# The variance of the decoder attention's row norm: root and reciprocal on two engines, or one power on GpSimd

## The reference, cut to what matters

```
x = _layernorm(x + _L1_attn_ref(x, ...), axis=-1)
x = _layernorm(x + _L1_xattn_ref(ctx_1024, ctx_1024, x, mask, ...), axis=-1)

def _layernorm(x, axis=-1, eps=1e-05):
    m = jnp.mean(x, axis=axis, keepdims=True)
    v = jnp.var(x, axis=axis, keepdims=True)
    return (x - m) / jnp.sqrt(v + eps)
```

## Time and profile before

| | |
|---|---|
| median of 3 runs | 3104.47 us (3103.09 to 3105.31) |
| profiled execution, first to last instruction (its span; no other time of it is listed) | 3103.9 us |
| PE busy | 2762.8 us, 89% of the span |
| DVE busy | 2047.4 us, 66% |
| ACT busy | 1633.0 us, 53% |
| POOL busy | 290.6 us, 9% |
| the stream in the span | about 1390 to 2653 us |
| mean granted TensorE clock over the span | 0.944 |

### The profile page before, as it was taken

The page is one execution under the profiler, slowest core; times in us unless marked ns, Lnnn a source line. Parts: engine busy times, 40 slices in busy tenths (PEclk is TensorE's granted clock), DMA queues, the critical chain, the costliest instruction groups (busy, mean ns, idle before and its releaser), DMA issues. The chain is left out here.

```text
span 3103.9 us, 86016 instructions
## 1 busy us (share of the span) xinstructions
PE 2762.8 (89%) x35706; PEld 1378.2 (44%) x35707; DVE 2047.4 (66%) x4208; ACT 1633.0 (53%) x3066; POOL 290.6 (9%) x413
## 2 busy tenths in 40 slices
PE   6798988999988987799999999999999999379993
PEld 3574643444544552233333333333343433256762
DVE  3443148888844247689898998989998984412224
ACT  2234223666662221477777777877777778023331
POOL 2117010010010010300000000000000000300003
PEclk9998988999999998799999999999999999589996
DMA  5413032101010013221121221111111110710112
GB/s 160 125 45 108 1 111 66 40 3 39 3 37 12 1 36 98 80 69 45 52 53 28 63 53 38 46 46 55 46 45 45 46 45 2 269 41 32 32 34 90
DMA packets 115181, 173.67 MB, mean 56 GB/s; under 512 B 20138, under 2 KB 90683, under 8 KB 114451
## 3 DMA queue, kind: packets, MB, share of 16 engines
q1 hardware_dynamic: 109012, 160.12, 18.0%
q0 software_dynamic: 5824, 8.49, 0.9%
HBM read 127.63 MB, written 40.51 MB: 54 GB/s over the span
## 5 line engine op out<-in xcount | busy, mean ns | idle before, releaser
L1390 DVE TENSOR_REDUCE d_part_max<-d_ps_m 128x1 f32<-128x512 f32 (+1 forms) x1964 | 1125.1, 631 | 77.1 <-PE d_ps_m L1377 52.6
L1707 ACT ACTIVATE d_prob<-d_ps_s 128x512 f32<-128x512 f32 x1856 | 960.7, 602 | 256.5 <-PE d_ps_s L1566 253.6
L1377 PE MATMUL d_ps_m<-k_st,q_st 97*32 97x512 bf16 (+1 forms) x5296 | 471.7, 361 | 0.0
L1566 PE MATMUL d_ps_s<-q_st,k_st 98*32 98x512 bf16 x5104 | 445.1, 385 | 23.3 <-ACT d_prob L1707 21.4
L776 DVE TENSOR_REDUCE x_part_max<-x_att_ps_m 128x1 f32<-128x512 f32 (+2 forms) x578 | 308.4, 587 | 42.7 <-PE x_att_ps_m L752 18.3
L1017 ACT ACTIVATE x_att_prob<-x_att_ps_s 128x1024 f32<-128x1024 f32 (+3 forms) x296 | 258.2, 921 | 131.0 <-PE x_att_ps_s L898 77.6
L1582 PE MATMUL d_ps_o<-d_prob,a_values 128*32 128x512 f32 x2048 | 265.3, 594 | 0.0
L1566 PEld LDWEIGHTS d_ps_s<-q_st,k_st 98*32 98x32 bf16 x5104 | 136.6, 96 | 278.8 <-ACT d_prob L1707 175.4
L1377 PE MATMUL d_ps_m<-q_st 97*32 97x512 bf16 (+1 forms) x2560 | 227.5, 361 | 0.0
L1377 PEld LDWEIGHTS d_ps_m<-k_st,q_st 97*32 97x32 bf16 x5296 | 141.4, 96 | 178.2 <-issue 67.4
L1582 PE MATMUL d_ps_o<-d_prob,x_values 128*32 128x512 f32 x1664 | 216.3, 595 | 0.2 <-ACT d_prob L1707 0.2
(11 more groups left out here) (328 smaller groups left out, 3339.7 us busy)
## 6 DMA issues: line engine op xcount, KB each, us to landing
k_st<-parts_k SPq DMA_DIRECT2D x90, 256.0 KB, 5.2
k_st<-parts_k SPq DMA_DIRECT2D x90, 208.0 KB, 4.6
l_w<-in_l_w SPq DMA_DIRECT2D x16, 1024.0 KB, 14.3
q_st<-parts_q SPq DMA_DIRECT2D x48, 256.0 KB, 4.6
q_st<-parts_q SPq DMA_DIRECT2D x192, 64.0 KB
q_st<-parts_k SPq DMA_DIRECT2D x30, 256.0 KB
q_st<-parts_k SPq DMA_DIRECT2D x30, 208.0 KB
parts_q<-a_proj_parts SPq DMA_DIRECT2D x16, 384.0 KB, 2.5
```

The source lines that it names most:

```text
L1377: mm = pe.matmul(bank[q:q + COLUMNS, 0:w], self.query(s, h, ROW_MASK + 1, a * P + q, COLUMNS), self.key(s, h, ROW_MASK + 1, k, w), start=T ...
L1390: dve.tensor_reduce(self.part[:, h * QT + a, i:i + 1], bank[:, 0:w], AX.X, ALU.max).then_inc(s_read, 1)
L1566: mm = pe.matmul(ps_s[n % len(ps_s)][k:k + COLUMNS, :], maxima.key(s, h, ROW_MAX + 1, kt * P + k, COLUMNS), maxima.query(s, h, ROW_MAX + 1 ...
L1707: act.activation(prob[:, p % 2, h, :], ps_s[n % len(ps_s)][:, :], ACT.Exp, scale=scale).then_inc(s_prob, 1)
```

## The change

The square root on ScalarE and the reciprocal on VectorE are replaced by two instructions on GpSimd: it adds eps to the variance (128x4, into a new tile `variance`), waits for its own result, and raises that to the power that a tile `power` holds, filled with -0.5 once at the start of the stage (`ALU.pow`, 128x4, into `inv`). The task `root` stands at the same pair of the list, in GpSimd's program now. The task `inverse` is gone. VectorE waits for the semaphore `inv` at the head of each `normalise_row`.

```diff
--- before.py
+++ after.py
@@ -1268,7 +1268,6 @@
                 self.tasks[start + 1 + a].append(("turn", k, a))
                 self.tasks[start + 2 + a].append(("prod", k, a))
             self.tasks[start + 7].append(("root", k))
-            self.tasks[start + 8].append(("inverse", k))
             for a in range(QT):
                 self.tasks[start + 8 + a].append(("scale", k, a))
                 self.tasks[start + 9 + a].append(("fm", k, a))
@@ -1461,15 +1460,16 @@
         parts = sb("parts", [P, 2, 3, QC], BF16)
         stat = sb("stat", [P, 2, QT, 6], F32)
         mean_var = sb("mean_var", [P, 2, QT, 2], F32)
-        std = sb("std", [P, 2, QT], F32)
+        variance = sb("variance", [P, QT], F32)
+        power = sb("power", [P, QT], F32)
         inv = sb("inv", [P, 2, QT], F32)
         ps_s = [ctx.enter_context(nc.psum_tensor(f"{name}_ps_s{i}", [P, QC], F32)) for i in range(3)]
         plan.set_ring([ctx.enter_context(nc.psum_tensor(f"{name}_ps_m{i}", [P, QC], F32)) for i in range(4)])
         ps_o = ctx.enter_context(nc.psum_tensor(f"{name}_ps_o", [P, QC], F32))
         s_scores, s_prob, s_pv, s_msc, s_mred, s_ocopy, s_turn, s_inv_den, s_norm = map(
             sem, ("scores", "prob", "pv", "msc", "mred", "ocopy", "turn", "inv_den", "norm"))
-        s_oturn, s_ofm, s_prod, s_base, s_y, s_stat, s_mv, s_std, s_inv, s_x, s_xturn, s_xfm = map(
-            sem, ("oturn", "ofm", "prod", "base", "y", "stat", "mv", "std", "inv", "x", "xturn", "xfm"))
+        s_oturn, s_ofm, s_prod, s_base, s_y, s_stat, s_mv, s_power, s_var, s_inv, s_x, s_xturn, s_xfm = map(
+            sem, ("oturn", "ofm", "prod", "base", "y", "stat", "mv", "power", "var", "inv", "x", "xturn", "xfm"))
         s_w, s_ctx, s_wo, s_pad, s_ones, s_mm, s_exact, s_high, s_rest, s_mid, s_low, s_vmm, s_vout = map(
             sem, ("w", "ctx", "wo", "pad", "ones", "mm", "exact", "high", "rest", "mid", "low", "vmm", "vout"))
         s_store = [sem(f"store{i}") for i in range(2)]
@@ -1717,11 +1717,6 @@
                 act.activation(o_fm[:, n % 2, :, :], plan.bank(step)[:, 0:D].rearrange("p (a b) -> p a b", a=DT),
                                ACT.Copy).then_inc(s_ofm, 1)
 
-            def root(k):
-                act.wait_ge(s_mv, QT * (k + 1))
-                act.activation(std[:, k % 2, :], mean_var[:, k % 2, :, 1], ACT.Sqrt,
-                               bias=cst["eps"][:, 0:1]).then_inc(s_std, 1)
-
             def copy_normed(step):
 
                 k, a = step[1:]
@@ -1756,8 +1751,6 @@
                 for task in plan.tasks[p]:
                     if task[0] == "turn":
                         copy_tokens(task)
-                    elif task[0] == "root":
-                        root(task[1])
                     elif task[0] == "fm":
                         copy_normed(task)
                     elif task[0] == "unit":
@@ -1779,6 +1772,19 @@
                 pool.tensor_tensor(x, x, bo_sb[:, si, :], ALU.add).then_inc(s_base, 1)
                 bases += 1
 
+            def root(k):
+
+                pool.wait_ge(s_mv, QT * (k + 1))
+                if k >= 1:
+                    pool.wait_ge(s_inv, k)
+                pool.tensor_scalar(variance[:, :], mean_var[:, k % 2, :, 1], EPS, None, ALU.add).then_inc(s_var, 1)
+                pool.wait_ge(s_var, k + 1)
+                if k >= 2:
+                    pool.wait_ge(s_x, QT * (k - 1))
+                pool.tensor_tensor(inv[:, k % 2, :], variance[:, :], power[:, :], ALU.pow).then_inc(s_inv, 1)
+
+            pool.memset(power[:, :], -0.5).then_inc(s_power, 1)
+            pool.wait_ge(s_power, 1)
             pool.memset(ctx_sb[:, :, CTX:CTXP], 0.0).then_inc(s_pad, 1)
             pool.memset(segments[1].values[:, :], 1.0).then_inc(s_ones, 1)
             pool.wait_ge(s_wo, 64)
@@ -1793,6 +1799,8 @@
                         if u >= 2:
                             pool.wait_ge(s_store[u % 2], 16 * (u // 2))
                         pool.tensor_copy(parts[:, u % 2, 1, 0:n], rest[:, 0:n]).then_inc(s_mid, 1)
+                    elif task[0] == "root":
+                        root(task[1])
                     elif task[0] == "base":
                         k, a = task[1:]
                         pool.wait_ge(s_xturn, k * QT + a + 1)
@@ -1838,13 +1846,9 @@
                 dve.wait_ge(s_stat, n + 1)
                 dve.bn_aggr(mean_var[:, k % 2, a, :], stat[:, k % 2, a, :]).then_inc(s_mv, 1)
 
-            def inverse(k):
-                dve.wait_ge(s_std, k + 1)
-                dve.reciprocal(inv[:, k % 2, :], std[:, k % 2, :]).then_inc(s_inv, 1)
-                dve.wait_ge(s_inv, k + 1)
-
             def normalise_row(k, a):
                 x = x_tok[:, tile(k, a), :]
+                dve.wait_ge(s_inv, k + 1)
                 dve.tensor_scalar(x, x, mean_var[:, k % 2, a, 0:1], inv[:, k % 2, a:a + 1], ALU.subtract,
                                   ALU.mult).then_inc(s_x, 1)
 
@@ -1884,8 +1888,6 @@
                 for task in plan.tasks[p]:
                     if task[0] == "prod":
                         add_product(task)
-                    elif task[0] == "inverse":
-                        inverse(task[1])
                     elif task[0] == "scale":
                         normalise_row(*task[1:])
                     elif task[0] == "unit":
```

## The result

The changed kernel takes 3082.69 us (median of 4 runs, 3079.64 to 3084.19), the kernel before 3104.89 beside it (3103.09 to 3106.8): ratio 0.9927, interval 0.9913 to 0.9941. That is 22.2 us less. The prediction was 3084 us, range 3079 to 3092.

What follows compares the result with a forecast made beforehand. TensorE was taken to bound the stream (98% busy), VectorE close behind. From 3103.9 us, less 15.95 for stalls and 5.94 for clock dips, plus 1.0 for VectorE's return and 1.0 for the last root: 3084 us, range 3079 to 3092.

Steps and rivals of the forecast that it cites:

- The stalls: TensorE's losses at the seven mid-stream roots: three at 2.37 and four at 2.21 us, 15.95 us removed.
- The clock: Lower clock behind four mid-stream roots, taken as caused by TensorE standing: two at 1.28 and two at 1.69, 5.94 us removed.
- rival 3: The clock's falls in mid-stream are not caused by TensorE standing, so 5.9 us stay: 3090 us, chance 8%.
- The return on VectorE: VectorE just fits behind each mid-stream root; 0.15 us a root comes back as TensorE waits for banks, +1 us.
- Rival 4: VectorE becomes the bound in the stream: 0.7 us a root comes back, 5 us in place of 1, 3088 us; chance 9%.
- GpSimd's price and cover: At mid-stream roots, 1 us for two GpSimd instructions and waits, hidden by 8.0 us before VectorE wants the result.
- Rival 2: GpSimd's power starts slowly; mid-stream hides it, the end of chunk 7 pays +5.4 us at T = 6: 3088.5 us, chance 10%.
- The last root: Behind chunk 7 all is in series; two GpSimd instructions replace 0.58 us: +1.0 us, between 0.2 less and 1.2 more.
- T - 0.6: Extra time behind chunk 7, with T the time of GpSimd's two instructions; from a rival of 5% chance.
- upper end of 1.2: Extra time behind chunk 7 if both GpSimd instructions cost as in the high row: 1.57 + 0.2 us.
- The sum: Whole kernel: 3103.9 - 15.95 - 5.94 + 1.0 + 1.0 = 3084.0 us.
- The rule of the Trainium skill: ScalarE table switches: about 1380 ns drain beyond the 1283 ns load, making the gain 19 us larger; not used.

Runs made afterwards that it cites:

- spare_sqrt: The changed kernel with ScalarE's square root back in all eight roots, written to a tile nobody reads: 3105.6 us, ratio 0.9998 to the kernel before.
- scalar_busy_long: The changed kernel with three spare 128x900 copies on ScalarE at each of the first seven roots, no table switch: 3103.25 us, ratio 0.9992 to the kernel before.
- spare_identity: The changed kernel with an unread identity on ScalarE in all eight roots, which needs no other table: 3082.92 us, ratio 0.9924 to the kernel before.
- vector_busy_x3: The changed kernel with three spare row statistics on VectorE ahead of the first normalisation of each of the first seven chunks: 3088.52 us, ratio 0.9938.
- x6: The changed kernel with six spare row statistics on VectorE ahead of the first normalisation of each of the first seven chunks: 3098.29 us, ratio 0.9969.
- power_x11: The changed kernel with ten spare GpSimd powers ahead of the one that counts, in each of the first seven roots: 3118.75 us, ratio 1.0042.

## Why the prediction was right

*The stalls.* Right in mechanism and size: 2.37 us at three roots and 2.21 at four were forecast, 2.37 and 2.27 measured, 16.2 in place of 15.95. The first table load alone would not have mattered so much: 1.57 us of ScalarE's time cost 0.76 or less, 2.9 cost 2.1 to 2.4.

*The clock.* Forecast 5.94 us from four dips, on the argument that each followed a stall. spare_sqrt and scalar_busy_long brought dips back with the stalls, spare_identity didn't. That leaves rival 3 without support. Which stall is followed by one varies: chunks 1, 2, 5, 6 before, 1, 2, 3, 4, 6 with the spare root. Forecast and measurement of the two together are 21.9 and 22.7. Of the difference 0.2 us is in the stalls and 0.2 in the third pair of chunk 0, which took 3.52 us before and takes 3.32 now. The other 0.4 is in the dips of chunks 1 and 2: the forecast's 1.28 is measured from chunk 0 with that longer third pair in it, and from the changed kernel each is 1.49. So the four dips that the forecast removed are what one trace of the kernel before had, and another execution may have more or fewer.

*The return on VectorE.* Forecast +1.0, measured none. This is the term that was off. I read VectorE's idle time in the stall (2.33 us against 2.21) as its whole reserve. With the stall gone VectorE still has 0.1 us to spare in the first segment and 0.55 in the second, as vector_busy_x3 and x6 showed. At chunk 0 there was a gain instead: in the kernel before, TensorE waited 0.34 us for VectorE in the third pair, and this wait is gone. In spare_sqrt, which has the stall and not the reciprocal, it is gone too (that root costs 2.35 us, in the kernel before 2.57), so it goes with the reciprocal and its wait. Rival 4 is out: TensorE's waits for VectorE in the stream fell from 2.9 to 2.2 us.

*GpSimd's price and cover.* Forecast 1 us for the two instructions and waits in mid-stream, 1.44 to 1.48 measured from the last variance to the result, and hidden either way. Forecast cover 8.0 us at chunk 3; in the changed kernel VectorE is ready for the result 7.9 us after the last variance there and 7.7 at chunks 0 to 2. Rival 2 is out: all eight powers take 1.04 to 1.05 us, the first as the last, though up to 184 us lie between them. The Trainium skill (GPSIMD Engine Reference, Instruction dispatch) has some 6 us for the first call of a freshly loaded kernel of that engine; the trace shows no such delay at the first power, and doesn't show whether anything was loaded for it.

*The last root.* Forecast +1.0, measured +0.90, and that is partly luck. The forecast's own 1 us for the two instructions would have given 1.0 - 0.6 = +0.4 by its formula T - 0.6; the +1.0 leaned on an upper end of 1.2 that was a guess about another operation. The power was slower than the addition of 64 times as many elements (1.04 against 0.785 us), so the row of 256 elements was no upper bound for it, and 1.48 us came out below the 1.77 of that end only because the addition of 128x4 takes 0.23.

*The sum.* -19.9 forecast from the span, -21.5 measured. Of the 1.6 us between them the 0.8 above, the return of 1.0 and the last root's 0.1 make 1.9; the closing's new dip, +2.5, and the -2.2 of the other stretches nearly cancel, and were in the range and not in the sum. That they cancel is luck too.

*The rule of the Trainium skill* on a drain behind each table load (ScalarE: Activation LUTs, What ACT_TABLE_LOAD costs) would have made the gain 19 us larger. With no loads left 22 us were gained and not 41, and with the root back in the spare_sqrt kernel the loads are again 1.28 us with the next instruction right behind. The trace decides for the load alone.

## What to carry to other kernels

A short instruction that needs another activation table cost two loads here, and it is priced by what ScalarE can be away before its consumer stands: 0.3 us cost nothing, 1.6 us 0.7, 2.9 us 2.0 to 2.4, in a kernel whose bounding engine had three banks of lead. Moving such an instruction to a slower engine is a gain if the result has cover there, so measure from the last operand to the first use (7.7 us here) and compare that with the new engine's time, and price the places without cover by themselves. When the engine that bounds is TensorE, read the granted clock behind every stall: in these traces the clock was about a quarter of the gain.

## What the runs showed of the hardware that I had not expected

- GpSimd's power on 128x1 takes 0.56 to 0.59 us, on 128x4 1.04 us; back to back ten of 128x4 take 9.84 us. A two-operand addition of 128x256 takes 0.785 us in the same kernels.
- How often the clock fell behind a stall went with the stall's length, by TensorE's idle time just ahead: none of 14 at 0.48 to 0.60 us and none of 4 at 0.83, two of three at 1.44, three of seven at 1.86 to 1.97, four and five of seven at 2.1 to 2.2, six of seven at 2.2 to 3.1. These are few stalls each, and in three of them the clock fell while TensorE still stood. The pauses of 0.8 to 1.1 us that the stream has anyway had no dip in any trace. A dip cost 1.3 to 1.7 us, and the three of double length in power_x11 about 2.9 each.
- A table load with nothing waiting ran ahead of the semaphore wait of its own activation: in the kernel before the last root's load began at 2646.01, 2.27 us before the variance that the root waits for was complete.
